# Where the value matmuls stand in a fused attention and gated feed-forward layer: from ten places of a group to six

## The reference

```
q, k, v = xn @ Wq + bq, xn @ Wk + bk, xn @ Wv + bv     # 16 heads of 16 channels, q and k rotated
att = softmax(causal((q k^T + bias[bucket(j - i)]) / 4))
attention = (att v) @ Wp + bp
logits = cosine(xn, col_emb) + sigmoid(gelu(xn @ gate_w1 + b) @ gate_w2 + b)   # 16 columns
ffn = layernorm((gelu(xn @ W_cols + b) * top1(softmax(logits))) @ proj_w + proj_b + xn) * ln_g + ln_b
```

## Time and profile before

| | |
|---|---|
| median of 3 runs | 1976.82 us (1974.98 to 1978.83) |
| the profiled execution | 1979.27 us, its span 1977.3 us |
| PE busy | 1810.0 us, 92% of the span |
| DVE busy | 1548.7 us, 78% |
| ACT busy | 1111.8 us, 56% |
| value matmuls (line 1189) | 3072, 317.5 us busy |
| PE clock granted, mean | 0.98 of full speed |

### The profile page before, as it was taken

One profiled execution on the slowest core, in us unless ns is written; L12 is line 12 of the kernel. 1 busy time (PEld: TensorE's weight loads), 2 busy tenths in 40 slices (PEclk: granted clock), 3 DMA queues, 4 the chain that ended last, 5 costly groups with the idle time before them and its releaser, 6 DMA issues.

```text
span 1977.3 us, 35087 instructions
## 1 busy us (share of the span) xinstructions
PE 1810.0 (92%) x10870; PEld 1041.7 (53%) x10870; DVE 1548.7 (78%) x5438; ACT 1111.8 (56%) x2150; POOL 783.6 (40%) x1018
## 2 busy tenths in 40 slices
PE   5779999999999999999999999999999999999877
PEld 3555555555556555555555555565555555555433
DVE  4568888878877887888887888787888788777783
ACT  3326555566655566665555666555666555655544
POOL 6553444343444344344434344433434443311110
PEclk9789999999999999999999999999999999999998
DMA  6673233333233323433333332332333232232201
GB/s 185 181 176 92 76 90 97 105 97 102 89 95 100 111 65 97 123 90 88 99 97 90 112 93 75 104 109 79 97 102 106 85 103 85 60 87 72 58 12 49
DMA packets 220469, 189.44 MB, mean 96 GB/s; under 512 B 63387, under 2 KB 195371, under 8 KB 220284
## 3 DMA queue, kind: packets, MB, share of 16 engines
q1 hardware_dynamic: 219840, 186.83, 33.4%
q10 hardware_dynamic: 444, 0.38, 0.1%
HBM read 118.64 MB, written 69.27 MB: 95 GB/s over the span
## 4 chain that ended last, share of the span: by engine, by line
PE 56%; DVE 26%; ACT 8%; issue 6%; DMA 1%; POOL 1%; SPq 1%; DVEq 0%; ACTq 0%; POOLq 0%
PE scores L1273 10%; PE rows L1210 10%; PE o_bank L1189 9%; PE scores L1172 8%; PE bank L1284 7%; DVE scores L1357 5%; DVE rows L1379 5%; DVE maxima L1384 5%; ACT probs L1051 4%; PE bank L1302 3%; PE bank L1234 3%; PE scores L1275 2%; DVE maxima L1379 2%; PE bank L1228 1%; DVE scores L1359 1%
## 5 line engine op out<-in xcount | busy, mean ns | idle before, releaser
L1051 ACT ACTIVATE probs<-scores 128x512 f32<-128x512 f32 (+1 forms) x1280 | 671.6, 555 | 511.6 <-DVE scores L1357 296.6
L1384 DVE TENSOR_REDUCE maxima<-rows 128x1 f32<-128x512 f32 (+4 forms) x896 | 479.9, 552 | 166.8 <-PE rows L1210 163.1
L1172 PE MATMUL scores<-stack_q,stack_k 99*128 99x512 bf16 (+3 forms) x1536 | 430.5, 331 | 79.3 <-ACT probs L1051 70.4
L1210 PE MATMUL rows<-stack_k,stack_q 96*128 96x256 bf16 (+3 forms) x2048 | 459.4, 290 | 15.8 <-DVE maxima L1379 6.8
L1379 DVE CUSTOM_DVE_ANT_0 rows<-rows,near_rows 128x256 f32<-128x256 f32 (+1 forms) x1024 | 394.5, 431 | 54.8 <-PE rows L1210 54.1
L1357 DVE TENSOR_TENSOR scores<-scores,near_cols 128x256 f32<-128x256 f32 x768 | 320.7, 430 | 67.6 <-PE scores L1172 67.4
L1210 PEld LDWEIGHTS rows<-stack_k,stack_q 96*128 96x128 bf16 x2048 | 175.0, 98 | 313.6 <-issue 112.8
L1189 PE MATMUL o_bank<-probs,v_aug 128*32 128x512 f32 (+3 forms) x3072 | 317.5, 501 | 2.8 <-ACT probs L1051 2.8
L1273 PE MATMUL scores<-again,w_cols 128*128 128x256 f32 x1024 | 275.2, 391 | 3.6 <-DMA b_cols<-in_b_cols_dram 3.6
L1172 PEld LDWEIGHTS scores<-stack_q,stack_k 99*128 99x128 bf16 x1536 | 139.9, 97 | 254.8 <-ACT probs L1051 195.7
L1284 PE MATMUL bank<-w_proj,act_t 128*128 128x256 f32 x1024 | 255.4, 382 | 14.6 <-DVE y L1414 14.2
(11 more groups left out here) (123 smaller groups left out, 2138.8 us busy)
## 6 DMA issues: line engine op xcount, KB each, us to landing
parts_d<-part SPq DMA_DIRECT2D x96, 256.0 KB, 2.2
stack_q<-parts_d SPq DMA_DIRECT2D x378, 64.0 KB, 3.1
stack_k<-parts_d SPq DMA_DIRECT2D x378, 64.0 KB, 2.3
kept_d<-kept SPq DMA_DIRECT2D x31, 512.0 KB, 2.9
again<-kept_d SPq DMA_DIRECT2D x31, 512.0 KB, 3.5
x<-in_x_dram SPq DMA_DIRECT2D x32, 256.0 KB, 3.4
turns<-turns_d SPq DMA_DIRECT2D x32, 256.0 KB, 3.0
v_d<-v SPq DMA_DIRECT2D x32, 256.0 KB, 2.4
```

Of the source, the lines that this page charges most:

```text
L1051: act.activation(probs[:, (g * NS + s) % PROBS, h, 0:width], ring[(rings + ring_n[1]) % RING][:, 0:width], ACT.Exp, scale=float(D) ** -0.5 ...
L1172: ins = pe.matmul(ring[(rings + ring_n[1]) % RING][:, c0:c0 + w], stack_k[g % 2][:, h, kb * P:(kb + 1) * P], stack_q[g % 2][:, h, q0:q0 + ...
L1210: ins = pe.matmul(tile[:, c0:c0 + k1 - k0], stack_q[ag % 2][0:STACK, h, qb * P:(qb + 1) * P], stack_k[ag % 2][0:STACK, h, k0:k1], start=Tr ...
L1384: ins = dve.tensor_reduce(maxima[:, part, m:m + n], tile[:, c0:c0 + n * w].rearrange("p (n w) -> p n w", w=w), AX.X, ALU.max)
```

## The change

`pv` 0 moves from slot 8 to 12, ahead of pv 1. pv 3 moves from slot 20 to 24, ahead of pv 4. pv 5 moves from slot 28 to 32, ahead of pv 6. pv 8 moves from behind slot 39 into the closing part, ahead of pv 9. The other six stay. The places of the rows are worked out anew by the same `with_rows` from the new order.

```diff
-PV_AFTER = 8
+PV_AT = {12: (0, 1), 16: (2,), 24: (3, 4), 32: (5, 6), 36: (7,)}
+PV_LAST = (8, 9)
...
-CLOSING = [("load", None), ("load_v", None), ("neurons", (0, 0)), ("neurons", (0, 1)), ("pv", NS - 1), ("o_out", 1),
+CLOSING = [("load", None), ("load_v", None), ("neurons", (0, 0)), ("neurons", (0, 1)), ("pv", PV_LAST[0]), ("pv", PV_LAST[1]), ("o_out", 1),
...
             plan.append(("score", (s, h)))
-            if i >= PV_AFTER and (i - PV_AFTER) % GH == 0:
-                done = (i - PV_AFTER) // GH
-                plan.append(("pv", done))
-                if done == LAST_STEP[0]:
-                    plan.append(("o_out", 0))
+            plan += [("pv", s) for s in PV_AT.get(i, ())]
+            if LAST_STEP[0] in PV_AT.get(i, ()):
+                plan.append(("o_out", 0))
...
-        plan += [("pv", s) for s in range((SLOTS - 1 - PV_AFTER) // GH + 1, NS - 1)]
```

## The result

The changed kernel takes 2131.95 us (median of 4 runs, 2123.74 to 2132.18), the kernel before 1977.22 us. The ratio is 1.0773, with a 95% interval of 1.0745 to 1.0801: 153 us slower. The forecast was 2052 us, its range ended at 2075 us. The sign was right, the size was half of what came.

What follows compares the result with a forecast made beforehand. PE carries most, but DVE and ACT set the pace in parts of each group. 2.1 us with projections, 3.0 without, mean 2.55 over 28 groups, plus 1 us for each of the last four: +75 us, 2052 us, range 2005 to 2072.

Steps and rivals of the forecast that it cites:

- What bounds: PE, DVE and ACT bound in turn; a pv ahead of a PE wait is free, one behind it delays what follows.
- S5.1's wait: Sign in the trace: PE's wait ahead of S5.1 becomes 1.3 us longer.
- ACT's idle time ahead of S6.1: Sign in the trace: ACT's idle time there becomes longer by 1 us.
- the wait directly ahead of S2.3: Sign in the trace: PE's wait there becomes about 1 us longer.
- The price of a place, and the joints: A place costs 0.23 us beside streaming; 20 new touching pairs save 4.6 us at most, counted as nothing.
- The rival from PE's total: PE sets the pace, only joints matter: 1972 us, or 1948 us with no rows between pairs; chance 0.10.
- pv 0, pv 3, pv 8: Lateness terms per group: 0.75 us at pv 2, +1.25 us from slot 24, 0 with or +0.9 us without projections at the end.
- L: How much later a thing starts than in the kernel before, counted within a group.
- The term of +0.1 us: pv 5, slot 28 to 32: later waits for ACT cover it, so +0.1 us; bounds -0.5 and +0.5.
- a row (0.2 us) that moves across the wait: At S2.3, in groups with projections, a replanned row lands behind the wait and adds 0.2 us.
- the sum, made at full clock: 28 groups at mean 2.55 us, last four at 1 us each: together +75 us.
- Slower still: Rival: each place also starves ACT, no wait shrinks: 3.4 us, 95 us, 2072 us; slower than the range had chance 0.04.

Runs made afterwards that it cites:

- e6: The changed kernel, but with_rows puts no row between two pv's that follow one another, so all pairs touch: ratio 1.0785.
- e12: The changed kernel with the unused matmuls of e5 and no row between two pv's: ratio 1.0591, 117 us over the kernel before.
- e5: The changed kernel with matmuls of unused results added in PE's waits in the first 28 groups: ratio 1.0605, 120 us over the kernel before.
- e4: The kernel before with only pv 8 moved, into the closing part ahead of pv 9, rows planned anew: ratio 1.0107, 21 us.
- e13: The kernel before with all four pv's moved as in the change, but every row kept at its old place: ratio 1.0472, 93 us.
- e15: The kernel before, all pv's at their old places, but rows where the changed order puts them: ratio 1.0223, 44 us.
- e10: The kernel before with only pv 5 moved to slot 32, unused matmuls in PE's waits, rows at their old places: ratio 1.0066, 13 us.
- e17: The kernel before; in groups without projections one row moves from ahead of the projection's second half to behind S3.0: ratio 1.0036, 7 us.
- e9: The kernel before with only pv 5 moved to slot 32, unused matmuls in PE's waits, rows planned anew: ratio 1.0150, 30 us.
- e16: The kernel before, meant to move the row directly ahead of S8.0 behind pv 6; no row was there, order unchanged: ratio 1.0007.
- e14: As e13, with unused matmuls added in PE's waits to hold its clock: ratio 1.0442, 87 us over the kernel before.
- e7: The kernel before with only pv 1 moved, from slot 12 to slot 10, rows planned anew: ratio 1.0006.
- e18: The kernel before with pv 1 moved from slot 12 to slot 10, every row kept at its old place: ratio 1.0001.

## Why the prediction was wrong, and what of it held

**What bounds.** Held. A pv moved behind a wait makes what follows late, though not by its whole 1.08 us where later waits take some of it in, and taken from ahead of a wait it gives nothing: S2.3 at 2.86 us and S5.1's wait longer by 1.3 us (1.51 against 0.19), ACT's idle time ahead of S6.1 1.31 us where it was none, the projection's wait 1.81 against 0.49. One sign came smaller than forecast: the wait directly ahead of S2.3 is 0.72 us instead of 0.50, and not 1 us longer; a new wait of 0.61 us for DVE, ahead of S2.1, has the rest of the time that pv 0 left.

**The price of a place, and the joints.** The starts are 1.00, 0.27 and 0.86 us for pv, row, pv, against the forecast 1.00, 0.26, 0.78. The prediction's working has a slip: from 1.00 and 0.78 us with 0.22 for each 128 columns 0.12 us are left, not 0.15, so a place costs 0.20 us and not 0.23. That changes nothing in the forecast, which counted the joints as nothing. This held nearly so even with all pairs touching: e6 is as the change, and e12 is some 3 us below e5. The rival from PE's total is out: 107 more joints at 0.20 us would be 21 us, and by the intervals e12 can have gained hardly more than 8. What the Trainium skill's page "TensorEngine Tiling (Array Packing)", section "Tiling Modes", states, that a change of mode drains TensorE, isn't touched by that. It is the gain in time that is out, not the drain.

**pv 0, pv 3, pv 8.** Forecast L 0.75, then +1.25, and 0 or +0.9. The changed kernel at full clock has 0.9, +1.3, and e4 0.2 and +1.1. The places are right, the sizes in part by luck. Without its row the forecast for pv 0 was 0.55 us, and with the rows kept it has 0.4 (e13); the rows alone make 0.9 at the same place (e15), where the forecast had 0.2. For pv 3 it was 1.05 without its row, and e13 has 0.9. The value matmuls were priced too high and the rows far too low, and the two errors met.

**pv 5.** The term of +0.1 us was near for the pv itself and wrong for its move. With rows kept and full clock L doesn't grow from slot 32 to 36 in groups with projections (1.2 and 1.2 in e13). e10 has 13 us for 28 groups, about half of it from the unused matmuls. With the rows moved and the clock free it is 55 us.

**The step that failed first: "a row (0.2 us) that moves across the wait".** The rows entered the sum with 0.2 us at slot 12, 0.2 at slot 24 and 0.1 on average at `neurons`: 28 x 0.5 = 14 of the 75 us. Alone they cost 44 us (e15). In the whole change they have 153 - 93 = 60 us with the clock free, and 120 - 87 = 33 us with it held. The prediction had counted where `with_rows` would put them, but priced them by PE's matmuls and not by the tile and DVE's maximum. e17 shows that price at one place. For the step at S9.0 the traces of e9 and e10 show that the rows make it; which row it is wasn't tried, since e16 moved none.

**The step that failed second: the sum, made at full clock.** It took all durations from a kernel whose clock fell only at its ends, and called the longer waits free. They were not: PE went into the projection behind S2.3 after 1.44 instead of 2.21 us of work and got 1.2 GHz for it. This is worth at least the 33 us between the change and e5, and more by what the unused matmuls in e5 cost.

**The account.** By runs: pv's new places with rows kept and clock held 87 us (e14), the rows' new places 33 us (e5 less e14), holding the clock 33 us (the change less e5), together 153 us. Less the 22 us that the unused matmuls cost by the estimate above, pv's new places have some 65 us, where the forecast without its rows was 75 - 14 = 61 us. That part of the sum held. If the unused matmuls cost as much in e5 as in e14, the clock has some 55 us. The 37 stretches at 1.2 GHz in the first 28 groups give the same, at 1.5 us each. Both are estimates, and the terms aren't fully separate: with the clock free the rows have 60 us, and the stretches at 1.2 GHz in the first 28 groups are 27 in e13 against 37. Of the 153 us the last four groups have some 10, where the forecast had 4.

**The rivals.** None of them named the clock or the rows' tile. "Slower still" had the right side of the forecast, by a reason (no wait shrinks) that the traces don't show: with the rows kept L was 0.4 us at S5.1 for a pv of 1.08.

No version here beats the kernel before: e7 and e18, the only ones that don't lose, are within 0.2% of it.

## What to carry to other kernels

In this kernel work that stood ahead of a wait cost nothing. Moved behind the wait it cost from nearly nothing (pv 5) to most of its length (pv 3), depending on the waits that still came. The wait that it leaves may not be free either: look at the matmuls that run next on TensorE and price them at the lower clock too. Matmuls added only to hold the clock have a price of their own, which must be taken off before the clock's part is read from them. If a planner places other work around what you move, price that work by what it holds (a tile, a turn of another engine), not by its own matmuls; and measure once with the planner's result frozen, before you credit or blame the move.

## What was not expected of the hardware

PE's clock falls inside the dense part of a kernel that is busy 88% of its span, for 3 us at a time. The two stretches from S2.0 to S2.3 shown above have the same 1.44 us of work in 2.95 us. Behind one of them the clock fell, behind the other it didn't. What decides between them isn't settled by any run here. With the waits filled (e5) it fell in no group from the second to the 27th.

The Trainium skill, page "TensorE: Matmul & The Clock Gate", section "Part 1: The HAM clock gate", states that the gate is set by how busy the array has been recently, and that the moments at which this is judged aren't tied to the kernel's start. The first agrees with e5. The second would allow two equal stretches to end differently; no run here tests it.
